# First batches reordered and the 3x3 convolution computed as three packed products

## The reference, cut to what matters

```python
# 32 images of 128 channels x 32 x 32; N = 1024 pixels (tokens) each
xn   = (x - mean_c) / sqrt(var_c + 1e-5) * ln_w + ln_b
bcdt = einsum('bchw,oc->bohw', xn, w_bcdt)                # 64 channels
bcdt = conv_general_dilated(bcdt, w_gw, padding 1, 3x3, feature_group_count=32)
BC, dt = split(bcdt.reshape(B, 64, N), 2, axis=1)
AB = softmax(dt + A[None, :, None], axis=-1) * BC
y  = w_out @ (einsum('bcn,bsn->bcs', x, AB) applied to BC) + x
t  = tokens(y)                                            # 1024 tokens x 128
t  = t + attention(layernorm(t))                          # one head, 64 units, 1024 x 1024 scores
t  = t + mixture_of_experts(layernorm(t))                 # 8 experts, top 1, capacity 5120, 128 -> 512 -> 128
```

## Time and profile before

| | us |
|---|---|
| three runs, median | 2148.56 |
| profiled execution | 2159.72 |
| its span, first to last instruction | 2157.5 |
| TensorE busy in the span | 1991.0 (92%) |
| VectorE busy | 1750.4 (81%) |
| ScalarE busy | 1196.4 (55%) |
| GpSimd busy | 1088.2 (50%) |

### The profile page before, as it was taken

How to read it: one execution, slowest core, us unless ns; L and a number is a source line. 1 busy time by engine, 2 the same in 40 slices (tenths; PEclk the granted TensorE clock), 3 DMA queues, 4 the chain that set the end, 5 groups by cost and what they waited for, 6 DMA issues and landing times. The chain is left out here.

```text
span 2157.5 us, 41952 instructions
## 1 busy us (share of the span) xinstructions
PE 1991.0 (92%) x13855; PEld 1639.8 (76%) x13855; DVE 1750.4 (81%) x5467; ACT 1196.4 (55%) x2216; POOL 1088.2 (50%) x1243
## 2 busy tenths in 40 slices
PE   1669999999999999999999999999839999999996
PEld 1347787877878788787887878877629998888985
DVE  2257888888888888888888888888739998888985
ACT  0135555555555555555555555555427777777773
POOL 3111445555545545455454554544436665555554
PEclk9679999999999999999999999999959999999997
DMA  4911221221212212122121221212137777777874
GB/s 164 397 40 32 58 70 50 57 74 51 70 50 57 74 51 69 51 56 74 53 67 50 57 74 54 63 39 54 39 111 204 205 234 259 259 242 256 244 244 172
DMA packets 163511, 243.97 MB, mean 113 GB/s; under 512 B 31039, under 2 KB 110478, under 8 KB 163296
## 3 DMA queue, kind: packets, MB, share of 16 engines
q1 hardware_dynamic: 146016, 209.46, 32.2%
q0 software_dynamic: 17280, 31.84, 4.5%
HBM read 115.95 MB, written 95.56 MB: 98 GB/s over the span
## 5 line engine op out<-in xcount | busy, mean ns | idle before, releaser
L1184 PE MATMUL pvp<-va,pT 128*128 128x129 f32 x4096 | 503.3, 275 | 0.4 <-ACT pT L727 0.3
L1184 PEld LDWEIGHTS pvp<-va,pT 128*128 128x128 f32 x4096 | 484.1, 191 | 21.5 <-issue 11.1
L641 POOL DMA_INDIRECT expert_slots<-rows,slot_i x256 | 378.0, 1476 | 99.3 <-issue 89.8
L1355 POOL DMA_INDIRECT token_rows<-res x284 | 308.8, 1087 | 231.8 <-DVE res L1488 162.3
L727 ACT ACTIVATE pT<-stp 128x512 f32<-128x512 f32 x512 | 293.1, 596 | 132.9 <-PE stp L1158 126.9
L839 DVE TENSOR_REDUCE mxs<-mxp 128x1 f32<-128x512 f32 x512 | 336.0, 683 | 37.6 <-PE mxp L1061 27.3
L1541 PEld LDWEIGHTS e_yp<-w2s,hid 128*128 128x128 f32 x2272 | 294.2, 192 | 20.3 <-ACT hid L1418 0.3
L1541 PE MATMUL e_yp<-w2s,hid 128*128 128x128 f32 x2272 | 299.9, 275 | 0.0
L1418 ACT ACTIVATE hid<-e_hp,b1c 128x512 f32<-128x512 f32 x284 | 195.3, 688 | 113.8 <-PE e_hp L1533 105.5
L1061 PE MATMUL mxp<-khi,qhi 127*128 127x512 f32 x512 | 218.4, 469 | 13.7 <-issue 11.2
L1156 PE MATMUL stp<-qhl,klh 128*128 128x512 f32 x512 | 223.5, 436 | 3.1 <-DMA qhi<-nt 1.9
(11 more groups left out here) (242 smaller groups left out, 3836.6 us busy)
## 6 DMA issues: line engine op xcount, KB each, us to landing
w1p<-w_parts SPq DMA_DIRECT2D x71, 512.0 KB
expert_slots<-fill SPq DMA_DIRECT2D x32, 660.0 KB, 11.3
e_rows<-expert_slots SPq DMA_DIRECT2D x71, 264.0 KB, 4.9
w2s<-in_w SPq DMA_DIRECT2D x71, 256.0 KB
xs<-in_x SPq DMA_DIRECT2D x32, 512.0 KB, 4.8
token_rows<-rows SPq DMA_DIRECT2D x32, 512.0 KB, 3.8
f_rows<-token_rows SPq DMA_DIRECT2D x32, 512.0 KB, 6.9
out<-f_cols SPq DMA_DIRECT2D x32, 512.0 KB, 7.5
```

The costliest lines, as they stand in the source:

```text
L641: g.indirect_dma_start(out=slots, out_offset=bass.IndirectOffsetOnAxis(ap=slot_i[k][:, t:t + 1], axis=0), in_=rows[k][:, t, :], in_offset= ...
L1184: last = mm(pvp[qt % 2][:, 0:VA], pT[c][:, kt, n * P:(n + 1) * P], va[k][:, kt, :], start=(kt == 0), stop=(kt == NT - 1))
L1355: g.indirect_dma_start(out=tokens, out_offset=bass.IndirectOffsetOnAxis(ap=res[n % 2][:, q, TOKEN:TOKEN + 1].bitcast(I32), axis=0), in_=re ...
```

## The change

- **Constants and loads in the order of need.** GpSimd first writes what the front of batch 0 needs and signals `ident_ready` and `early_ready`; the rest (`state_constants`, `late_constants`) it writes behind its `xs` step of batch 0. SP issues x, six loads (`w_first`) and the next x. The twelve other loads are issued by ScalarE. Each engine waits for the late ones where it first uses them.
- **The taps** are turned by TensorE behind `x_turn` of batch 0, and copied by VectorE behind the statistics of batch 0, into space that lies in `pT[0]`.
- **The experts' weight parts** are moved from the start to the `xs` step of batches 4 to 11, one expert in each; their store and the next load go to SP's `x_turn` one batch later.
- **The fill** is issued by ScalarE: 16 transfers of 1.35 MB, two at a time, ahead of the steps `bT_turn`, `dt`, `cd_turn`, `u1_turn`, `qk`, `qk_high` of batch 0 and `bT_turn`, `dt` of batch 1, from space in `pT[1]`; ScalarE waits for their end before it writes `pT[1]` the first time.
- **The convolution** is 18 packed matmuls instead of 6 plain ones. A new step `img_split` makes the two parts of the image.
- **The lists** `head`, `steps` and `tail` are new. `head` now takes batch 0 to its first `mx` steps before `conv` of batch 1.

```diff
-        steps = [("t1b", 0), ("g", 2), (("mx", 0, 7), 1), (("st", 1, 7), 0), (("negmax", 0), 1), ("y", 2),
+        steps = [("ln2m", -1), ("t1b", 0), ("ln2g", -1), ("conv", 2), ("dt", 2), ("dt_exp", 2), (("mx", 0, 0), 1),
...
+                if st == "img_split":        # ScalarE
+                    act.wait_ge(s["imgt_ready"], b + 1)
+                    if not first:
+                        act.wait_ge(s["conv_done"], b)
+                    a.copy(imgh[:], imgt[:]).then_inc(s["imgh_ready"], 1)
...
+                if st == "img_split":        # VectorE
+                    dve.wait_ge(s["img_ready"], b + 1)
...
+                    v.tensor_scalar(imgt[:].bitcast(I32), img[:].bitcast(I32), HIGH_BITS, None, ALU.bitwise_and)\
+                        .then_inc(s["imgt_ready"], 1)
...
+                    v.tensor_tensor(imgl[:], img[:], imgt[:], ALU.subtract).then_inc(s["imgl_ready"], 1)
...
                 if st == "conv":             # TensorE
-                    for d in range(2):
-                        for kh in range(3):
-                            last = mm(work[:, 0, :], wtap[:, d, kh, :], img[:, kh:kh + H, d:d + W // 2],
-                                      start=(d == 0 and kh == 0), stop=(d == 1 and kh == 2))
+                    for n, (w_part, i_part) in enumerate(((wtaph, imgh), (wtapl, imgh), (wtaph, imgl))):
+                        if n == 2:
+                            pe.wait_ge(s["imgl_ready"], b + 1)
+                        for d in range(2):
+                            for kh in range(3):
+                                last = mm(work[:, 0, :], w_part[:, d, kh, :], i_part[:, kh:kh + H, d:d + W // 2],
+                                          start=(n == 0 and d == 0 and kh == 0), stop=(n == 2 and d == 1 and kh == 2))
...
                 if st == "xs":               # VectorE
                     stats(xT, bn, mv, s["x_stats"], s["x_rstd"], b)
+                    if first:
+                        taps()
+                    if W1_FIRST <= b < W1_FIRST + E:
+                        w1_part(b - W1_FIRST)
...
+                if st in ("bT_turn", "dt", "cd_turn", "u1_turn", "qk", "qk_high") and filled[0] < NFILL:   # ScalarE
+                    fill_slots()
```

More of the change, by code:

```diff
@@ L237, in batch @@
         def batch(b):
             return b, b // 2, b % 2
-        head = [(0, "x_turn"), (0, "xs"), (0, "bcdt"), (0, "bT_turn"), (0, "conv"), (0, "dt"), (0, "dt_exp"),
[40 rows of a table removed]
-                (4, "bT_turn"), (2, ("negmax", 1)), (2, ("pv", 0, 2)), (2, ("mrow", 1)), (3, "mask"), (4, "conv"),
[13 rows of a table removed]
-                (3, ("pv", 0, 2)), (3, ("mrow", 1)), (4, "qk_lrelu"), (4, "mask"), (2, ("ln2n", 3)), (5, "conv"),
[14 rows of a table removed]
-                (4, ("pv", 0, 2)), (5, "qk_lrelu"), (5, "mask"), (4, ("mrow", 1)), (6, "conv"), (5, "qk_high"),
[14 rows of a table removed]
-                (6, "qk_lrelu"), (6, "mask"), (5, ("mrow", 1)), (7, "conv"), (4, ("ln2n", 3)), (6, "qk_high"),
[5 rows of a table removed]
@@ new lines, in token_program @@
+        tail = [(8, "ln2m"), (7, "t1b"), (8, "ln2g"), (5, "conv"), (5, "dt"), (5, "dt_exp"), (6, ("mx", 0, 0)),
[12 rows of a table added]
+                (5, "qk_lrelu"), (7, ("ln2n", 2)), (6, ("negmax", 1)), (4, "img_split"), (6, ("pv", 0, 1)),
+                (5, "mask"), (6, ("pv", 0, 2)), (6, ("mrow", 1)), (7, ("ln2n", 3)), (5, "qk_high"), (4, "conv"),
[27 rows of a table added]
+                (4, ("mx", 1, 6)), (4, ("mx", 1, 7)), (3, "qk_lrelu"), (2, "bT_turn"), (2, "img_split"),
+                (5, ("ln2n", 1)), (4, ("negmax", 1)), (5, ("ln2n", 2)), (5, ("ln2n", 3)), (4, ("pv", 0, 1)),
+                (3, "qk_high"), (4, ("pv", 0, 2)), (4, ("mrow", 1)), (3, "mask"), (5, "ln2m"), (3, "qk_low"),
[13 rows of a table added]
+                (3, ("mx", 1, 7)), (3, ("negmax", 1)), (1, "img_split"), (3, ("pv", 0, 1)), (2, "mask"),
+                (4, ("ln2n", 2)), (4, ("ln2n", 3)), (2, "qk_lrelu"), (2, "qk_high"), (3, ("pv", 0, 2)), (4, "ln2m"),
+                (3, ("mrow", 1)), (2, "qk_low"), (1, "conv"), (1, "dt"), (1, "dt_exp"), (4, "rowid"),
[31 rows of a table added]
+                (1, "pos"), (1, "scatter")]
@@ L583, in _ @@
             chain(g.memset(img[:], 0.0))
[L584 to L589 removed]
+            g.memset(neghalf[:], -0.5).then_inc(s["early_ready"], 1)
+            pool.wait_ge(s["early_ready"], 1)
@@ new lines, in _, with state_constants @@
+            chain(g.memset(pairs[:], 0.0))
+            for d in (U - S, U, U + S):
+                chain(g.affine_select(out=pairs[:], in_=pairs[:], pattern=[[-1, U]], compare_op=ALU.not_equal, fill=1.0,
+                                      base=-d, channel_multiplier=1))
+            chain(g.memset(fill[:], 0.0))
+            g.memset(fill[:, :, TOKEN:TOKEN + 1].bitcast(I32), NO_TOKEN).then_inc(s["fill_ready"], 1)
+            def state_constants():
+                chain(g.memset(ident2[:], 0.0))
+                for d in range(2):
+                    for j in range(Q4):
+                        own = ident2[:, d * S:(d + 1) * S]
+                        ins = g.affine_select(out=own, in_=own, pattern=[[-1, S]], compare_op=ALU.not_equal, fill=1.0,
+                                              base=-j * S, channel_multiplier=1)
+                        if (d, j) == (1, Q4 - 1):
+                            ins.then_inc(s["state_ready"], 1)
+                        else:
+                            chain(ins)
@@ L811, in _ @@
-            last.then_inc(s["taps_ready"], 1)
-            dve.wait_ge(s["wcen_psum"], 1)
-            v.tensor_tensor(wcen[:], wln[:], work[:, 1, 256:256 + U], ALU.subtract).then_inc(s["wcen_ready"], 1)
-            v.tensor_copy(cbias[:], work[:, 1, 384:385]).then_inc(s["cbias_ready"], 1)
-            v.tensor_tensor(gwc[:, 0:E], gw_s[:], work[:, 1, 448:448 + E], ALU.subtract).then_inc(s["gwc_ready"], 1)
-            for e in range(E):
-                w1_part(e)
+            dve.wait_ge(s["wcen_psum"], 1)
```

273 lines of the change are left out of this document (154 added, 119 removed), and 356 rows, old and new, of tables (head, steps, tail).

## The result

The changed kernel takes 2138.8 us (median of 12 runs, 2131.6 to 2143.9); the kernel before took 2151.6 us in the same rounds (12 runs, 2144.9 to 2157.8). The ratio is 0.9939, 95% interval 0.9925 to 0.9952. It is faster, by 13 us and not by 64, and the time lies 21 us above the top of the 2066 to 2118 us that the prediction spans. The two profiled executions (2159.72 and 2134.68 us) are 25 us apart, which overstates the gain. In them the last scatter of the first program starts at 1591.8 and 1574.8 us, 17 us sooner; from there to the end it is nearly all the experts, which no kernel here changes, and this took 557.6 to 567.9 us in the profiled executions of all kernels of this document.

The account below looks back on a forecast made before the run. TensorE was taken to bound the steady state, with about 84 us idle in the head. Head 43 plus convolution 26.7 minus tightness 6 gave 64 us, so 2148.6 - 64 = 2085 us; range 2071 to 2099, with rivals B and C 2066 to 2118.

Parts of the forecast that it names:

- Part 3, the head: First batches: earlier loads and new order start convolution 0 at 24 us, v of batch 1 at 110.4; gain 43 us.
- rival C: Head: the fill holds up ScalarE or batch 0's transfers, the head gains 20 us less, 2105 us; chance 0.12.
- Part 1, the convolution: 30 dense batches: packed matmuls at 0.2325 us take 4.73 us instead of 5.62, saving 0.89 per batch, 26.7 us.
- the tightness: Steady state: loss from VectorE's fuller load and the longer path to conv, 0.2 us per batch, 6 us in all.
- Rival D: Convolution: packed matmul or its weight load misses 0.2325 us; at 0.43 the kernel takes 2188 us; chance 0.05.
- Part 2: img_split in the steady state: path to conv 1.1 us longer but covered by a pv step; loss 0.2 us per batch.
- Rival B: Steady state: VectorE or the path to conv becomes the bound, period stays about 44.9 us, 2106 us; chance 0.16.
- E: Batches 4 to 11: a third of w1 or order effects goes wrong, both gains shrink below what can be told; chance 0.05.
- room of VectorE (41.3 of 44.0 us): Batches 4 to 11: a w1 pair adds 1.12 us to VectorE, which still fits in the period.

Follow-up runs that it names:

- plain_conv_wait: Changed kernel with the convolution in plain float32, without img_split, and GpSimd's t1b waiting for VectorE's qkl of the next batch: 2144.4 us.
- t1b_after_qkl: Also called the wait kernel: changed kernel with GpSimd's t1b waiting for VectorE's qkl of the next batch, in the repeated part's 20 batches: 2118.1 us.
- short_split: t1b_after_qkl with VectorE's two img_split operations cut to one image row from batch 3 on: 2121.3 us.
- best: t1b_after_qkl with GpSimd's wait in batches 1 to 27 and the w1 pairs in batches 1 to 8, whole computation: 2114.6 us.
- before_collide: Kernel before the change with qk_low moved behind the step (mx 0 4) in the repeated part: 2165.9 us.
- pv_between: t1b_after_qkl with one pv step moved between bcdt and bT_turn in the repeated part: 2187.0 us.

## Why the prediction was wrong

**Part 3, the head, was right.** 24.25, 65.12 and 106.97 us against 24, 69 and 110.4: 45 us gained against 43. ScalarE's `u1n` of batch 0 starts at 46.7 us (48 in the forecast) and its waits up to 110 us are for TensorE, VectorE and once for GpSimd, so the fill did not hold it up and rival C did not happen. Not all of the 45 us lasted: at the convolution of batch 6 the gain is 41.5 us (298.94 against 340.46), where the forecast had 43 and some 3 us of packed products on top. Batches 4 and 5 already carry w1 pairs.

**Part 1, the convolution, was right in sum, with some luck.** Packed products and split together are worth 0.71 us a period (plain_conv_wait against t1b_after_qkl) where I had 0.89 - 0.2 = 0.69. But the parts are off in opposite directions. The product on rows of 16 out of 17 costs 0.247 us and not 0.2325, so the convolution and the two `mx` behind it take 4.99 us (898.81 to 903.80) and not 4.73, against 5.62 before: 0.63 saved and not 0.89. And VectorE's share of `img_split` costs nothing (short_split) where I had 0.2 for the tightness. The 0.08 us between 0.63 and 0.71 are not explained. Rival D, 0.43 us per product, did not happen.

**Part 2 failed, as the place where I priced the new order.** It said that the path to `conv` is covered by a second `pv` step and took 0.2 us for all tightness, with bounds of 0 and 1.22. I compared the steps around `conv`, and took the rest of the repeated part to run as in the earlier trace rows without asking of each moved step what now stands beside it on the *other* engines. The order of the repeated part had no term of its own in the sum, and only the rivals B and E spoke of it, E without a mechanism. Between the convolutions of batches 6 and 31 the changed kernel needs 1149.2 us (298.94 to 1448.18); before, 1122.5 (340.46 to 1462.93). My 25 x 0.69 would have made it 1105.2. The missing 44 us:

- 19 us: `qkl` stands behind GpSimd's `t1b` (1149.2 against 1130.3 in the wait kernel). I had no rival for this, and its price lies outside my bounds: 1.5 us in each long period. The rule of the Trainium skill quoted above names exactly this kind of pair; I had not held the neighbours in the new order against it.
- about 16 us: the new order itself, 0.66 us a period (plain_conv_wait), of which 0.2 are the chain `bcdt`, `bT`, `bT_turn`.
- about 7 us: the w1 pairs. In the wait kernel the five periods from batch 6 on take 46.31, 47.06, 45.86, 45.89 and 45.95, 6.9 us more than five of 44.83, and `best` gets 6.0 of them back. I had counted them as room of VectorE (41.3 of 44.0 us).
- about 2 us: the last three periods, behind the repeated part, in the tail's order (46.21, 44.98 and 45.69 us). This was not tried by itself.

Rival B's period of about 44.9 us is what the wait kernel has, 44.84, but by chance: not because VectorE is full or because `conv` waits, but because the order takes back what the products gain. The changed kernel itself needs more than B said, 45.8 us in the mean behind the w1 pairs. The sign of the forecast was right, by the head; its size was not.

## What to carry to other kernels

When steps are moved, list for each engine what will stand beside each step on the others. A VectorE operation with two SBUF inputs beside a GpSimd operation that reads SBUF has no dependency that would show, appears only as a longer duration, and can cost more than the whole edit gains. Compare the durations of *unchanged* operations in the two profiles by minimum and maximum, and where one has grown, look for who runs at the same time; a wait that keeps the two apart can be a gain. And before a step is moved as cover, ask what it covers now.

## What the runs showed of the hardware

- GpSimd's issue of an indirect DMA is slowed by VectorE as well. From 540 to 1320 us of the changed kernel, 51 issues had a VectorE operation on 1024 columns with inputs in SBUF alone beside them for at least 0.86 us and took 1.71 to 2.78 us; the 85 others took 0.97 or 0.98, beside PSUM reads, reductions or nothing alike (33 of them touch such an operation for at most 0.11 us). Before it was the same: 0.97 or 0.98 for 84, 0.97 to 3.83 for the 52 others. That is why `t1b` came sooner in before_collide: with `qkl` gone from beside the scatter, the issue there took 1.55 us instead of 3.83, and `t1b` started about 8.5 us behind the convolution instead of 10.6.
- The irregular change of long and short periods in the changed kernel comes mostly from the landing of the last scatter. From 578 to 1312 us its last issue ends 6.05 us behind the convolution in 15 of 16 periods. In the ten long ones `t1b` starts 1.4 us behind that, ahead of `qkl` (7.9 us behind the convolution); in five of the six short ones it has to wait for the landing for 1.85 to 2.4 us and starts level with `qkl` or behind it. In the sixth, the one shown above at 862.66, the issues themselves ended 1.3 us later. Why a landing takes longer is open.
- The Trainium skill, "SBUF — State Buffer", section "Who interferes with whom", says that a probe saw `tensor_copy` hold up a DMA, but not `tensor_tensor`, and gives as an inferred reason that `tensor_tensor` takes only the read side of the ports that the two engines share, while making descriptors needs the write side. The traces here differ for the indirect DMA:

```profile
899.53 2.78 POOL L644 DMA_INDIRECT expert_slots<-rows,slot_i  x1 [0.30 <-issue]
902.62 0.97 POOL L644 DMA_INDIRECT expert_slots<-rows,slot_i  x1 [0.30 <-issue]
```

  The first stands beside the two `tensor_tensor` of `ln2m` and `ln2g` (900.25 to 902.72 us), the second touches their last 0.1 us.
- A TensorE wait of 1.3 us in a dense stretch was followed by some 3 us at a granted clock of 0.51 (pv_between), which doubled its price; but in six of the 15 periods with the same wait the clock stayed at 1.00. The wait of 1.32 us for `abT` in the changed kernel had no such sequel either: the granted clock of its steady state stays at 1.00. So the length of the wait alone does not decide it, and what does was not tried.
